# A new order for the first batch of a fused attention and LoRA-FFN kernel

## The reference

```python
x = L0_attn_x                                   # 8 x 1024 x 256, float32
xn = layernorm(x)                               # (x - mean) / sqrt(var + 1e-5), no weights
q = xn @ wq.T + bq;  k = xn @ wk.T + bk;  v = xn @ wv.T + bv
attn = softmax(einsum('bqd,bkd->bqk', q, k) * 256**-0.5)
attention = einsum('bqk,bkd->bqd', attn, v)
lilora_weight = up_aux @ (lora_up @ (lora_down @ down_aux))
ffn = einsum('bsi,oi->bso', xn, W) + b + einsum('bsi,oi->bso', xn, lilora_weight)
out = x + attention + ffn
```

## Time and profile before

| | us |
|---|---|
| median of 3 runs (515.43 to 515.94) | 515.86 |
| the profiled execution | 516.27 |
| its span, first to last instruction | 514.5 |
| PE busy | 503.9 |
| POOL busy | 372.9 |
| DVE busy | 367.5 |
| ACT busy | 276.6 |

### The profile page before, as it was taken

One profiled execution on the slowest core, in us unless ns is written; L12 is line 12 of the kernel. 1 busy time (PEld: TensorE's weight loads), 2 busy tenths in 40 slices (PEclk: granted clock), 3 DMA queues, 4 the chain that ended last, 5 costly groups with the idle time before them and its releaser, 6 DMA issues.

```text
span 514.5 us, 8100 instructions
## 1 busy us (share of the span) xinstructions
PE 503.9 (98%) x2948; PEld 446.3 (87%) x2948; DVE 367.5 (71%) x839; ACT 276.6 (54%) x589; POOL 372.9 (72%) x221
## 2 busy tenths in 40 slices
PE   4999999999999999999999999999999999999997
PEld 4777897989989898898989989898998989889897
DVE  4789876876679585895858767686757758476594
ACT  2755677265754747367382665736474462725450
POOL 2843795986879966999669978699688976671730
PEclk9999999999999999999999999999999999999999
DMA  8020005000050002200050100501003010000002
GB/s 241 38 83 0 1 4 203 1 41 2 1 204 1 41 1 85 121 2 41 1 189 17 43 2 0 205 1 42 0 22 103 1 42 1 41 1 2 41 1 82
DMA packets 8694, 25.04 MB, mean 49 GB/s; under 512 B 1850, under 2 KB 3792, under 8 KB 7760
## 3 DMA queue, kind: packets, MB, share of 16 engines
q1 hardware_dynamic: 7328, 24.38, 13.1%
q10 hardware_dynamic: 1328, 0.16, 0.2%
HBM read 16.15 MB, written 8.39 MB: 48 GB/s over the span
## 4 chain that ended last, share of the span: by engine, by line
PE 96%; DMA 1%; ACT 1%; DVE 1%; issue 0%; ACTq 0%; DVEq 0%
PE o_ps L1080 12%; PE o_ps L1079 11%; PE o_ps L1078 11%; PE g_ps L998 10%; PE g_ps L999 10%; PE g_ps L1000 10%; PE s_ps L998 9%; PE s_ps L999 8%; PE s_ps L1000 8%; DMA bk_col<-in_L_attn_bk 1%; PE o_ps L998 1%; PE g_ps L1020 1%; PE o_ps L1000 1%; PE o_ps L999 1%; ACT prod L607 1%
## 5 line engine op out<-in xcount | busy, mean ns | idle before, releaser
L507 POOL TENSOR_TENSOR p_lo<-s,p_hi 128x1024 fp32r<-128x1024 f32 x60 | 143.8, 2429 | 38.8 <-ACT p_hi L657 38.8
L650 ACT ACTIVATE s<-s,e 128x512 f32<-128x512 f32 x128 | 84.3, 714 | 116.2 <-DVE s L848 116.1
L1080 PE MATMUL o_ps<-v_lo,p_hi 128*128 128x256 f32 x480 | 136.1, 283 | 0.0
L1079 PE MATMUL o_ps<-v_hi,p_lo 128*128 128x258 f32 x480 | 135.1, 282 | 0.0
L1078 PE MATMUL o_ps<-v_hi,p_hi 128*128 128x258 f32 x480 | 134.6, 281 | 0.0
L1078 PEld LDWEIGHTS o_ps<-v_hi,p_hi 128*128 128x128 f32 x480 | 91.3, 190 | 1.7
L1079 PEld LDWEIGHTS o_ps<-v_hi,p_lo 128*128 128x128 f32 x480 | 91.1, 190 | 1.6
L1080 PEld LDWEIGHTS o_ps<-v_lo,p_hi 128*128 128x128 f32 x480 | 90.2, 188 | 0.0
L807 DVE SCALAR_TENSOR_TENSOR tile_max<-s_ps,e,tile_max 128x512 f32<-128x512 f32 x80 | 59.9, 749 | 32.7 <-PE s_ps L1000 30.6
L998 PE MATMUL s_ps<-xt_hi,zt_hi 128*128 128x512 f32 x192 | 74.9, 390 | 0.0
L999 PE MATMUL s_ps<-xt_lo,zt_hi 128*128 128x512 f32 x192 | 74.7, 389 | 0.0
(11 more groups left out here) (157 smaller groups left out, 989.2 us busy)
## 6 DMA issues: line engine op xcount, KB each, us to landing
out<-base SPq DMA_DIRECT2D x15, 512.0 KB, 2.7
x_sb<-in_L_attn_x SPq DMA_DIRECT2D x7, 1024.0 KB, 8.2
x_t<-in_x_t SPq DMA_DIRECT2D x6, 1024.0 KB, 6.0
x_sb<-in_L_attn_x SPq DMA_DIRECT2D x4, 256.0 KB, 6.5
out<-base SPq DMA_DIRECT2D x4, 128.0 KB, 1.9
s<-in_L_attn_wk SPq DMA_DIRECT2D x1, 256.0 KB, 3.0
s<-in_L_attn_wq SPq DMA_DIRECT2D x1, 256.0 KB, 5.7
s<-in_L_attn_wv SPq DMA_DIRECT2D x1, 256.0 KB, 7.1
```

What stands on the lines that cost most here:

```text
L507: nc.gpsimd.tensor_tensor(p_pair(g, p_lo_sb, j), s_pair(j), p_pair(g, p_hi_sb, j).bitcast(f32), ALU.subtract).then_inc(p_lo_made, 1)
L650: nc.scalar.activation(s[:, n, :], s[:, n, :], ACT.Exp, bias=e[b % 2][:, n:n + 1]).then_inc(p_made, 1)
L1079: nc.tensor.matmul(o[:, 0:D + ONES], lo, v_hi[i][:, n, 0:D + ONES], start=False, stop=False)
L1080: mm = nc.tensor.matmul(o[:, 0:D], hi, v_lo[i][:, n, :], start=False, stop=last)
```

## The change

The head is written anew, and the first batch and the second change their form.

- PE waits for the identity first and transposes it 24 times (`WARM`) into a bank that nobody reads.
- One load brings the small vectors (`small`, packed by the host) in place of four transfers of single words. The first rows of x are loaded ahead of wk; wv comes earlier.
- `a` is made by plain float32 matmuls, without the split of wk and wq.
- Batch 0 goes by pairs of tiles: statistics in three stages, a transpose of two tiles (`turn`), V of a pair (`first_v`), z, scores; the FFN is a group of its own behind the scores (`first_ffn`), which ACT copies to `base[1]` and DVE adds.
- EARLY is 1: batch 1 is no longer transposed on PE but loaded transposed and normalised on POOL as batches 2 to 7 are.
- The stat rows of batch 2 are made by DVE at another place in chunk g=1.

```diff
-    EARLY = 2
+    EARLY = 1
+    STAGES = ((0, 2), (2, 4), (4, 8))
...
-        V_GROUPS = {0: (8, 9), 1: (10, 11), 2: (12, 13), 3: (14, 15)}
-        FIRST = [{0: (0, 1), 1: (2, 3), 2: (4, 5), 3: (6, 7)}, V_GROUPS]
-        LATER = [{1: (4, 5), 2: (6, 7)}, V_GROUPS]
+        V_GROUPS = {0: (4, 5), 1: (6, 7), 2: (8, 9), 3: (10, 11)}
+        FIRST_PLACES = [{2: (0, 1), 3: (2, 3)}, V_GROUPS]
+        PLACES = [{1: (0, 1), 2: (2, 3)}, V_GROUPS]
...
+            load_first(0)
+            sp.dma_start(wk_sb, rows(wk)).then_inc(wk_loaded, DMA)
+            load_first(1)
+            sp.dma_start(wq_sb, rows(wq)).then_inc(wq_loaded, DMA)
+            sp.dma_start(wv_t_sb, rows(wv_t)).then_inc(wv_loaded, DMA)
+            load_first(2)
+            load_first(3)
...
             load(1)
+            load_t(1)
             load(2)
...
             for b in range(B):
 
                 make_p_lo(CHUNKS * b)
                 if b == 0:
-                    make_rstd(EARLY, 0)
+                    make_xt_lo(1, 0)
+                    norm_x_t(1, 1)
+                    make_xt_lo(1, 1)
                 shift_raw(CHUNKS * b + 1)
...
-                if b + 1 < EARLY:
-                    make_prod(b + 1)
+                make_raw_prod(b + 1)
+                if b == 0:
+                    make_e_raw(1)
+
+                    pool.wait_ge(first_ffn_added, PAIRS)
+                make_x_bias(b + 1)
+                if b == 0:
+                    make_rstd(2)
                 else:
-                    make_raw_prod(b + 1)
-                if b == 0:
-
-                    pool.wait_ge(ffn_hi_made, 1)
-                make_x_bias(b + 1)
-                if b + 1 >= EARLY:
                     make_e_raw(b + 1)
                 make_p_lo(CHUNKS * b + 1)
...
             for g in range(LAST):
...
-                if b + 2 < B and c == 1:
-                    make_stat_row(b + 2, 0)
-                make_tile_max(g + 1, 0)
-                make_tile_max(g + 1, 1)
-                if b + 2 < B and c == 1:
-                    make_stat_row(b + 2, 1)
+                if 0 < b < B - 2 and c == 1:
+                    make_stat_row(b + 2, 0)
+                if g > 0:
+                    make_tile_max(g + 1, 0)
+                    make_tile_max(g + 1, 1)
+                if 0 < b < B - 2 and c == 1:
+                    make_stat_row(b + 2, 1)
...
                 make_groups_lo(b, c, 1)
+                if g == 1:
+                    make_stat_row(2, 0)
+                    make_stat_row(2, 1)
...
+            pe.wait_ge(identity_made, 1)
+            for _ in range(WARM):
+                nc.tensor.transpose(s_ps[2][:, 0:PT], identity[:, :], identity[:, :])
...
+            make_a(0)
+            turn(1)
+            make_a(1).then_inc(a_mm, 1)
+            first_v(0)
+            first_v(1)
...
+            first_z(0)
...
+            first_z(1)
+            turn(2)
+            turn(3)
...
-            for n in range(1, TILES):
+            scores(0, 0)
+            first_v(2)
+            scores(0, 1)
+            first_z(2)
+            first_z(3)
+            for n in range(2, TILES):
                 scores(0, n)
-            pe.wait_ge(wv_lo_made, 1)
-            pe.wait_ge(ffn_lo_made, 1)
-            pe.wait_ge(ones_made, 2)
-            for n in range(TILES):
-                group(0, 2 * NT + n)
+            for j in range(PAIRS):
+                first_ffn(j)
+            first_v(3)
```

More of the change, by code:

```diff
@@ L274, in two, with pair, group_bank, rstd_count @@
             return ap.rearrange("p (t n) -> p t n", t=DT)
[L276 to L281, removed]
-            if b == 0:
-                return o_ps[k % 2]
-            return g_ps[k % 2]
[L286 to L296, removed]
+        def pair(ap):
+            return ap.rearrange("p (m n) -> p m n", m=2)
+        TURN_BANKS = (g_ps[0], g_ps[1], g_ps[1], s_ps[3])
+        FIRST_V_BANKS = (o_ps[0], g_ps[0], o_ps[0], o_ps[0])
+        FIRST_Z_BANKS = (s_ps[0], s_ps[1], o_ps[0], o_ps[1])
+        FIRST_FFN_BANKS = (o_ps[0], o_ps[1], o_ps[0], o_ps[1])
+        RANK_BANK = s_ps[3]
+        WARM = 24
+        def group_bank(k):
+            return g_ps[k % 2]
+        def rstd_count(b):
+            return len(STAGES) + b
+        def stage_of(tile):
+            return [first <= tile < end for first, end in STAGES].index(True)
+        def prods(b):
+            return PAIRS * (b + 1)
+        def pair_of_columns(j):
+            return slice(2 * j * PT, (2 * j + 2) * PT)
         LAST = CHUNKS * B - 1
@@ L348, in _, with load_first @@
         def _(sp):
-            sp.dma_start(wk_sb, rows(wk)).then_inc(wk_loaded, DMA)
-            for j in range(4):
+            def load_first(j):
                 n = TILES // 4
@@ L532, in _ @@
                                     ALU.subtract).then_inc(ffn_lo_made, 1)
-            make_rstd(1, 0)
+            make_x_bias(0)
+            norm_x_t(1, 0)
             shift_raw(0)
@@ L573, in _ @@
-            act.dma_start(down_aux_sb, down_aux).then_inc(lora_loaded, DMA)
-            act.dma_start(up_aux_t, up_aux_t_in).then_inc(lora_loaded, DMA)
-            def make_xn(b, tiles):
-                act.wait_ge(shift_rstd_made, rstd_count(b, tiles[0] * 2 // TILES))
-                wait(act, group_mm, NG * (b - 1) + NT if b else 0)
-                wait(act, prod_made, TILES // 2 * b)
-                for n in tiles:
-                    nc.scalar.activation(xn[:, n, :], x_sb[b % 2][:, n, :], ACT.Identity,
-                                         bias=shift_rstd[b % 2][:, n:n + 1], scale=rstd[b % 2][:, n:n + 1]).then_inc(xn_made, 1)
+            act.dma_start(small[:, :], small_in).then_inc(small_loaded, DMA)
@@ L681, in _ @@
+            make_xn(4)
+            act.wait_ge(b_parts_made, 1)
+            first_z_hi(0)
+            make_xn(6)
+            act.wait_ge(mid_rank_mm, 1)
+            nc.scalar.activation(mid_rank, RANK_BANK[0:UDIM, D:2 * D], ACT.Copy).then_inc(mid_rank_made, 1)
+            first_z_hi(1)
+            turned_hi(2)
+            turned_hi(3)
+            make_e_sum(0, range(0, 4))
+            first_v_hi(2)
+            make_e_sum(0, range(4, TILES))
             make_e(0)
```

539 lines of the change are left out of this document (300 added, 239 removed).

## The result

The changed kernel takes 531.4 us (median of 4 runs, 529.86 to 533.12), the kernel before 515.9 beside it (4 runs, 515.43 to 516.39). The ratio is 1.0303, 95% interval 1.029 to 1.0315: slower by 15.5 us. The forecast was 522.6 with a range to 528.0. Its direction was right, its size was not. The profiled execution took 531.28 us, its span is 529.4.

The account below looks back on a forecast made before the run. PE sets the end, only 3.2 us ahead of POOL, whose strictly ordered queue would then bind: -0.4 (P) + 10.3 (idle) - 1.35 (rest) - 1.83 (reserve) = +6.7 us, so 522.6 us; range 518.0 to 528.0.

Parts of the forecast that it names:

- The head: Start to chunk 0's `top`: small-transfer wait and wk/wq split go, 24 transposes come; `top` at 41.6 instead of 44.3 us.
- top(0): When chunk 0's `top` is there: 41.6 us forecast, bounds 40.6 and 46, against 44.3 before.
- A wait for ACT's copy ... 1.3 (0 to 4): POOL, after batch 1's `norm_x_t`, waits for ACT's copy behind four chunk 1 exponentials: 1.3 us, 0 to 4.
- rival B: DVE's additions wait for POOL, or PE stays at the lower clock until 16: +9 to +12.5 us; chance 0.29.
- A wait for ACT's row sums and make_e_raw 1.65: POOL, after the products for e: wait for ACT's row sums plus `make_e_raw`, 1.65 us, of which `make_e_raw` alone 0.7.
- P: End of chunk 1's `p_lo` on POOL: forecast 41.6 + 51.1 = 92.7 us, against 93.1 before.
- POOL idle of 10.3 us from P: After chunk 1's `p_lo`, POOL idles 10.3 us because `norm_x_t(2)` needs batch 2's stat rows from DVE.
- "about 2 us" and "3 us": PE's waits before chunk 1's `p_lo` end: about 2 us for x plus bias, 3 us for the last `p_lo` pairs.
- POOL's rest 1.35: POOL's idle time before chunk 2's `p_lo` at 113.69 in the kernel before, 1.35 us, forecast to be used up.
- PE's reserve of 1.83: In the kernel before, POOL finishes chunk 2's `p_lo` 1.83 us before PE wants the fourth pair; subtracted from the delay.
- From chunk 3 on the same distances: Sign of being right: from chunk 3 on, PE is ahead of POOL by as much as before; the shift stays.
- Rival D: Faster: the stat-row wait doesn't bind, chunk g=0 begins at 43.6; -6.7, 509.2 us; chance 0.10.

Follow-up runs that it names:

- one-SBUF-input kernel: Changed kernel with DVE's three first-FFN additions reading a PSUM score bank instead of `base[1]`, FFN of six batch 0 tiles left out: 527.84 us.
- kept-busy kernel: Changed kernel with 28 more identity transposes on PE while it waits for the first FFN additions, ahead of chunk 0's first p x V: 533.9 us.
- rows earlier: Changed kernel with batch 2's two stat rows made by DVE behind chunk 2's last `tile_max`, not behind place 1's V groups: 523.14 us.
- before, rows late: Kernel before with only batch 2's stat rows moved to the changed kernel's late place, behind place 1's V groups in chunk g=1: 525.2 us.
- rearranged: Changed kernel with FFN additions split up, batch 1's x plus bias and ACT's copy for POOL earlier, stat rows ahead of chunk 2's `top`: 513.71 us.
- both-undone kernel: Changed kernel with a PSUM operand for the three FFN additions and batch 2's stat rows behind chunk 2's last `tile_max`: 518.42 us.

## Why the size was off, step by step

- **The head** was right in kind: PE's first product began at 6.18 (7 forecast, after the transposes), `shift_raw` of chunk 0 at 42.74 (top(0) at 41.6 forecast, `shift_raw` "at 41 to 43"). `top` was there at 42.59, 1.0 us late against the sum.
- **"A wait for ACT's copy ... 1.3 (0 to 4)"** is the step that failed most: it was 5.30. The prediction had named the cause as its rival B, "DVE's additions wait for POOL", and left it out of its sum. The one-SBUF-input kernel shows it: there the wait is 1.23. DVE's additions waited for POOL's `p_lo`, chunk 1's `top` came late by that, and ACT's exponentials and the copy behind them too. The rule of the Trainium skill that was weighed there ("SBUF — State Buffer", "Who interferes with whom"), that a DVE instruction with two SBUF inputs contends with a GpSimd instruction reading SBUF, is borne out by 2.2 to 2.7 us against 0.67.
- **"A wait for ACT's row sums and make_e_raw 1.65"**: 3.4 (79.78 to 83.16), 1.7 too small, in the changed kernel and in the one-input kernel alike. The row named for it (142.96 in the earlier trace rows) shows an idle time of 3.27 although x plus bias stands ahead of it there; where the 1 us of waiting in the 1.65 comes from, the prediction doesn't say. In the changed kernel ACT begins its eight row sums at 79.11 only, behind its copies of z, and takes 3.3 us for them.
- So **P** was 99.52 for 92.7, 6.8 more: 1.0 (head) + 4.0 + 1.7, and 0.1 of small ones.
- **"POOL idle of 10.3 us from P"** for the stat rows: 10.25. This term was right, and the two moves of the rows confirm it: earlier, the idle time is gone (-8.3 us by the medians); late in the kernel before, it is 11.82 (+9.5 us), there for DVE's own queue. The waits of PE on the way, "about 2 us" and "3 us", were 1.73 and 2.70 (1.34 + 1.36).
- **POOL's rest 1.35 and PE's reserve 1.83** held. With P at its measured value the sum is 6.4 (P against 93.1) + 10.25 - 1.35 - 1.83 - 0.4 (POOL's work in chunk 2 was that much shorter) = +13.1.
- **What the sum had no term for**: the lower clock level behind PE's waits. The stretch behind PE's last wait (138 to 143 us) costs 1.7 us: +14.8, where the spans differ by 14.9. From the forecast's own +6.7 it is 6.8 for P, 1.7 for the clock and 0.4 back for POOL's work. The prediction spoke of the lower level only at the start of the head. Only what is lost behind the last wait counts; the stretch at 60 to 64 was covered by the waits that follow, as the kept-busy kernel showed.
- **"From chunk 3 on the same distances"**: PE's waits end at 138.33, and with the stretch at the lower level, at 143, the whole difference of the spans is there.

PE's last wait and the clock behind it account for every kernel that waits. In the table "later" is the end of PE's last wait against the same product before (94.64 in chunk 1, 125.09 in chunk 2), "clock" what the lower level costs behind it, summed over stretches of 1 us; all in us, from the profiled executions.

| kernel | last wait ends | later | clock | sum | difference of the spans |
|---|---|---|---|---|---|
| changed | 138.33 | 13.2 | 1.7 | 14.9 | 14.9 |
| one SBUF input | 133.35 | 8.3 | 1.6 | 9.9 | 9.7 |
| rows earlier | 99.91 | 5.3 | 2.9 | 8.2 | 8.0 |
| both | 94.86 | 0.2 | 1.7 | 1.9 | 1.9 |
| before, rows late | 132.52 | 7.4 | 0 | 7.4 | 7.5 |
| PE kept busy | 141.80 | 16.7 | 2.5 | 19.2 | 19.1 |

Rival B at +9 to +12.5 was nearest, and even its upper end was 3 us short, since it priced neither the e wait nor the clock: with 1.7 for each, its +11.9 would be +15.3, against the 15.5 measured. Rival D, faster, exists as a kernel: the rearranged one, at 513.7 rather than 509.2. There chunk g=0 begins at 45.39 and not at D's 43.6, and PE still has waits of 0.7 and 1.7 us behind it.

## What to carry to other kernels

Before an instruction is moved to another place in an engine's order, ask who stands in a strict queue behind it: two small transposes on DVE, moved back by some 25 us, cost 7 to 10 us because POOL's whole next chunk waited behind one instruction. Where DVE and POOL work side by side, let DVE take one operand out of PSUM; an addition of 128x512 then costs 0.68 us, and up to 2.8 otherwise. And price a new wait of PE above its length: where the clock fell at the last wait on the path, it cost 1.6 to 2.9 us more. Warming PE up pays only where PE's own work sets the time behind it: 3.4 us in the rearranged kernel, nothing in the kernel before, where PE then waits for DVE.

## What the runs showed of the hardware that was not expected

- DVE's additions of 128x512 with both inputs in SBUF end 0.3 to 0.6 us after the POOL instruction that runs beside them; POOL itself loses little: two `p_lo` beside them took 5.25 us, and 4.81 in the rearranged kernel; an `xt_lo` took 2.82, and 2.41 there.
- The granted clock fell in or behind PE waits of 0.8 to 3.9 us, but not at every one: in the both-undone kernel it fell behind the wait that ended at 94.86 and not behind the 1.73 us that ended at 83.69, and the rearranged kernel kept its full clock through waits of 1.42 and 1.73 us. A whole stretch cost 1.7 us in some places and 3.4 in others (rows earlier, 58 to 65 and 98 to 106 us). What decides between these, the runs don't tell. The runs of one slower kernel lie 1.6 to 4.5 us apart, with mean clocks as far apart as 0.987 and 0.997, where the rearranged one stays within 0.8 in 12 of its 13 runs.
- With 24 transposes of 128x128 from 1.5 us on, the product for `e_row` behind them took 1.03 us at 6.18 in the changed kernel and 1.28 at 6.70 in the kernel before; without them 2.04 to 2.08.
